# A gated attention and quantised FFN block on one core: the hidden activations of the down product are transposed by DMA instead of by TensorE, with the order of TensorE's work rewritten around it

## The reference

```
x = x + tanh(g_xattn) * xattn(layernorm(x), ctx, ctx)
x = x + tanh(g_ffn)   * ffn(layernorm(x))

xattn: 8 heads of 64. Gates ig, fg from [q, k, v] @ kernel + bias; 
       log_D = cumsum(log_sigmoid(fg)) differences + ig, causal;
       D = exp(log_D - rowmax);  C = (q @ k.T / 8) * D
       h = C / (max(|sum C|, exp(-rowmax)) + eps) @ v;  h = h * rsqrt(mean(h^2) + 1e-6)

ffn:   bitlinear(x, w) = act_quant(x) @ weight_quant(w).T
       act_quant:    per token, round(x * 127 / max|x|) / scale        (whole numbers up to 127)
       weight_quant: round(w / mean|w|) clipped to -1, 0, 1
       g, u = bitlinear(x, w_gate), bitlinear(x, w_up)                  (512 -> 2048)
       h = relu(g)^2 * u
       y = bitlinear(h, w_down)                                        (2048 -> 512)
```

## Time and profile before

| | |
|---|---|
| median of 3 runs | 717.63 us (717.2 to 719.25) |
| the profiled execution | 714.83 us |
| its span | 713.1 us |
| PE busy | 657.5 us, 92% |
| DVE busy | 569.6 us, 80% |
| ACT busy | 424.6 us, 60% |
| POOL busy | 97.9 us, 14% |
| moved by DMA | 63.61 MB, 24.5% of the 16 DMA engines' time on SP's queue |

### The profile page before, as it was taken

One profiled execution on the slowest core, in us unless ns is written; L12 is line 12 of the kernel. 1 busy time (PEld: TensorE's weight loads), 2 busy tenths in 40 slices (PEclk: granted clock), 3 DMA queues, 4 the chain that ended last, 5 costly groups with the idle time before them and its releaser, 6 DMA issues.

```text
span 713.1 us, 13601 instructions
## 1 busy us (share of the span) xinstructions
PE 657.5 (92%) x4245; PEld 436.8 (61%) x4324; DVE 569.6 (80%) x1288; ACT 424.6 (60%) x893; POOL 97.9 (14%) x170
## 2 busy tenths in 40 slices
PE   8895877999999999999999999999999999999797
PEld 5682455575766666574757666665757576666433
DVE  3348756798898979797988979797988889796966
ACT  4254967756656665757566565657575565656542
POOL 1145220110101010101001010101010010101000
PEclk8557767999999999999999999999999999999999
DMA  9904600404113040504031130405040311402000
GB/s 314 382 20 177 206 1 1 163 17 143 37 56 123 15 162 0 177 0 163 15 126 52 49 128 15 162 0 177 0 163 15 117 60 36 143 16 75 2 30 29
DMA packets 45161, 63.61 MB, mean 89 GB/s; under 512 B 1872, under 2 KB 26704, under 8 KB 45136
## 3 DMA queue, kind: packets, MB, share of 16 engines
q1 hardware_dynamic: 43024, 61.19, 24.5%
q10 hardware_dynamic: 2112, 2.11, 0.9%
HBM read 54.77 MB, written 8.52 MB: 89 GB/s over the span
## 4 chain that ended last, share of the span: by engine, by line
PE 46%; DVE 24%; issue 16%; ACT 10%; DMA 2%; POOL 1%; DVEq 1%; SPq 0%; ACTq 0%; POOLq 0%
PE gb L1028 9%; PE ub L1028 8%; PE yb L1051 5%; PE ab L1061 5%; PE tp L1072 3%; PE tp L1074 3%; PE tp L1073 3%; DVE stage L717 3%; DVE dmat L820 2%; DVE ssq L838 2%; PE tp L1097 2%; ACT dmat L524 2%; DMA xs<-in_x 2%; DVE amax L879 2%; PE ab L1039 2%
## 5 line engine op out<-in xcount | busy, mean ns | idle before, releaser
L1028 PE MATMUL gb<-wgT,xqT 128*128 128x512 bf16 x480 | 132.0, 391 | 7.4 <-ACT xqT L505 5.5
L1051 PE MATMUL yb<-wdT,stage 128*128 128x512 bf16 x483 | 134.1, 380 | 2.8 <-ACT stage L498 2.1
L1028 PE MATMUL ub<-wuT,xqT 128*128 128x512 bf16 x497 | 134.2, 388 | 1.8 <-DVE stage L717 0.9
L484 ACT ACTIVATE relu<-gb 128x512 f32<-128x512 f32 x128 | 75.6, 591 | 32.7 <-PE gb L1028 31.7
L717 DVE TENSOR_TENSOR stage<-relu,ub 128x512 f32<-128x512 f32 x128 | 86.1, 682 | 5.3 <-ACT relu L486 5.3
L420 POOL TENSOR_SCALAR_AFFINE_SELECT dmat<-dmat 128x256 f32<-128x256 f32 x128 | 50.0, 415 | 285.1 <-ACT dmat L524 285.1
L1028 PEld LDWEIGHTS ub<-wuT,xqT 128*128 128x128 bf16 x512 | 50.2, 100 | 61.4 <-issue 6.2
L1051 PEld LDWEIGHTS yb<-wdT,stage 128*128 128x128 bf16 x512 | 59.5, 119 | 43.0 <-ACT stage L498 2.0
L532 ACT ACTIVATE ysb<-tp 128x260 f32<-128x260 f32 x64 | 24.8, 387 | 98.0 <-PE tp L1074 98.0
L486 ACT ACTIVATE relu<-relu 128x512 f32<-128x512 f32 x128 | 80.7, 630 | 4.1
L1028 PEld LDWEIGHTS gb<-wgT,xqT 128*128 128x128 bf16 x512 | 48.3, 103 | 54.2 <-issue 8.4
(11 more groups left out here) (114 smaller groups left out, 1090.8 us busy)
## 6 DMA issues: line engine op xcount, KB each, us to landing
dmat<-max_rows SPq DMA_DIRECT2D x14, 1024.0 KB, 5.0
values<-in_ctx_v SPq DMA_DIRECT2D x16, 520.0 KB, 7.5
xs<-in_x SPq DMA_DIRECT2D x16, 512.0 KB, 5.7
cT<-in_ctx_t SPq DMA_DIRECT2D x16, 512.0 KB, 6.7
out<-stage SPq DMA_DIRECT2D x32, 256.0 KB, 2.1
stage<-in_w_gate SPq DMA_DIRECT2D x4, 1024.0 KB, 12.8
stage<-in_w_up SPq DMA_DIRECT2D x4, 1024.0 KB, 17.8
stage<-in_w_down SPq DMA_DIRECT2D x4, 1024.0 KB, 5.2
```

The lines of the kernel that those rows point to most:

```text
L484: nc.scalar.activation(relu[:, c % 2, :], gb[c % 2][:, :], ACT.Relu).then_inc(g_free, 1)
L1028: last = nc.tensor.matmul(bank[c % 2][:, :], xqT[par][:, t, d, :], w[:, d, c * CH:(c + 1) * CH], start=(d == 0), stop=(d == KD - 1))
L1051: done = nc.tensor.matmul(yb[:, :], hqT[:, c, :], wdT[:, c, :], start=(c == 0), stop=(c == KF - 1))
```

## The change

`hq` of a token half is transposed by one DMA that SP issues (`turn_hidden`), [128, 2048] f16 into `hqT[t]`, [128, 16, 128] f16; there are now two tiles `hqT`, one for each half. TensorE's `hidden_transposes` and both `hidden_cols` go. The offset of 1536 stays in `hqT`, and so each `down` begins with one more product, of a tile `offset` (its first row is -1536, the rest 0) with `wsum`, the sums of the columns of `wdT`. `wsum` is made once in step 0, by 16 products with a tile of ones and a copy by ACT (`weight_sums`). DVE's `quantise_hidden` now also waits until the transfer of the half before has read `hq`, and SP's transfer waits for the second of the two quantising instructions and for the `down` that last read its `hqT[t]`.

The order is rewritten with it: TensorE issues all four chunks of a half before it goes on to the products of `down`; for the first half the transposes of q come between chunks (1, 2) and (1, 3), and the 16 gate products stand together between the two halves of `down` instead of one by one among its products. DVE's `output(b, 0)` and the last chunk's multiplication change places with neighbours. In SP's program each transfer stands ahead of the store of the same half.

The diff:

```diff
--- before
+++ after
@@ -134,7 +134,10 @@
         ot = [stage[1][:, FF * 2 + 2 * CH + D * t:FF * 2 + 2 * CH + D * (t + 1)] for t in range(T)]
-        hqT = stage[1][:, FF * 3:FF * 3 + FF // 2].bitcast(BF16).rearrange("p (k s) -> p k s", s=P)
+        hqT = [stage[1][:, FF * 3:FF * 3 + FF // 2].bitcast(F16).rearrange("p (k s) -> p k s", s=P),
+               sb("hqT1", [P, KF, P], F16)]
+        wsum = sb("wsum", [P, D], F16)
+        offset = sb("offset", [P, P], F16)
         hmaxes = sb("hmaxes", [P, T, 2], F32)
...
@@ -357,6 +356,15 @@
+            def turn_hidden(b, t):
+
+                sp.wait_ge(quant_step, QUANT_K * (2 * b + t) + QUANT_K - 1)
+                if not at(b, 0):
+                    alone(sp, sp_passed)
+                    sp.wait_ge(y_full, 2 * b + t - 1)
+                alone(sp, sp_passed)
+                sp.dma_start_transpose(hqT[t][:, :, :], hq[:, :]).then_inc(hq_turned[t], 16)
+
@@ -372,7 +380,9 @@
                 if not at(b, 0):
+                    turn_hidden(b - 1, 1)
                     store(b - 1, 1)
+                turn_hidden(b, 0)
                 store(b, 0)
@@ -380,6 +390,7 @@
             schedule(sp, step)
+            turn_hidden(LAST, 1)
             store(LAST, 1)
...
@@ -490,13 +504,10 @@
-            def hidden_cols(b, t):
-
-                act.wait_ge(a_full[0], hidden_use(b, t) + 1)
-                if not (at(b, 0) and t == 0):
-                    act.wait_ge(y_full, 2 * b + t)
-                nc.scalar.activation(hqT[:, 0:KF // 2, :], abh[0].rearrange("p (k s) -> p k s", s=P), ACT.Copy,
-                                     bias=-MAGIC16).then_inc(a_free[0], 1)
+            def weight_sums():
+
+                act.wait_ge(wsum_full, 1)
+                nc.scalar.activation(wsum[:, :], yb[:, :], ACT.Copy).then_inc(wsum_ready, 1)
@@ -626,8 +637,6 @@
                     magnitudes(2, 0, 4)
-                if prev:
-                    hidden_cols(b - 1, 1)
                 relu_square(b, 0, 2)
@@ -660,10 +669,10 @@
                 relu_square(b, 1, 1)
-                hidden_cols(b, 0)
                 if third:
...
                     sign_weight(2, 3, 4)
+                    weight_sums()
                 if n is not None:
@@ -672,14 +681,13 @@
                     quantise_second(n)
+                relu_square(b, 1, 3)
                 if m is not None:
                     forget_gate(m)
-                relu_square(b, 1, 3)
                 if n is not None:
...
             schedule(act, step)
-            hidden_cols(LAST, 1)
@@ -741,18 +749,14 @@
                     dve.wait_ge(winv_step, WINV[2] + 1)
+                elif t == 0:
+                    dve.wait_ge(hq_turned[1], 16 * b)
+                else:
+                    dve.wait_ge(hq_turned[0], 16 * b + 16)
                 for e in range(2):
...
-
-            def hidden_cols(b, t):
-
-                dve.wait_ge(a_full[1], hidden_use(b, t) + 1)
-                if not (at(b, 0) and t == 0):
-                    dve.wait_ge(y_full, 2 * b + t)
-                nc.vector.tensor_scalar(hqT[:, KF // 2:KF, :], abh[1].rearrange("p (k s) -> p k s", s=P), MAGIC16, None,
-                                        ALU.subtract).then_inc(a_free[1], 1)
@@ -985,22 +986,20 @@
                     quantise_tokens(n, npar)
+                hidden(b, 1, 3)
                 if m is not None:
                     gates_in(m)
+                hidden_max(b, 1, 0)
+                if m is not None:
+                    log_forget(m)
                     output(b, 0, par)
-                    log_forget(m)
-                hidden_max(b, 1, 0)
-                if m is not None:
                     cumulative(m, par)
-                hidden(b, 1, 3)
-                if m is not None:
                     running_max(m, par)
...
             schedule(dve, step)
-            hidden_cols(LAST, 1)
             output(LAST, 1, LAST % 2)
@@ -1029,30 +1028,28 @@
-            def hidden_transposes(b, t):
-                use = hidden_use(b, t)
-                for e in range(2):
-                    pe.wait_ge(quant_step, QUANT_K * (2 * b + t) + QUANT_K - 2 + e)
-                    pe.wait_ge(a_free[e], use)
-                    for s in range(KF // 2):
-                        piece = e * KF // 2 + s
-                        last = nc.tensor.transpose(abh[e][:, s * P:(s + 1) * P], hq[:, piece * P:(piece + 1) * P], identh[:, :])
-                    last.then_inc(a_full[e], 1)
-
-            def down(b, t, first, last, between=None):
+            def weight_sums():
+
+                pe.wait_ge(winv_step, WSUM[2])
+                for c in range(KF):
+                    if c % KD == 0:
+                        pe.wait_ge(w_ready[2], c // KD + 1)
+                    last = nc.tensor.matmul(yb[:, :], warm[:, 0:P], wdT[:, c, :], start=(c == 0), stop=(c == KF - 1))
+                last.then_inc(wsum_full, 1)
+
+            def down(b, t, first, last):
                 for c in range(first, last):
-                    if c == 0 and not (at(b, 0) and t == 0):
-                        pe.wait_ge(o_ready, 2 * b + t)
-                    if c % (KF // 2) == 0:
-                        pe.wait_ge(a_free[c // (KF // 2)], hidden_use(b, t) + 1)
-                    if at(b, 0) and t == 0 and c % KD == 0:
-                        pe.wait_ge(w_ready[2], c // KD + 1)
-                    done = nc.tensor.matmul(yb[:, :], hqT[:, c, :], wdT[:, c, :], start=(c == 0), stop=(c == KF - 1))
+                    if c == 0:
+                        if at(b, 0) and t == 0:
+                            pe.wait_ge(wsum_ready, 2)
+                        else:
+                            pe.wait_ge(o_ready, 2 * b + t)
+                        nc.tensor.matmul(yb[:, :], offset[:, :], wsum[:, :], start=True, stop=False)
+                        pe.wait_ge(hq_turned[t], 16 * b + 16)
+                    done = nc.tensor.matmul(yb[:, :], hqT[t][:, c, :], wdT[:, c, :], start=False, stop=(c == KF - 1))
                     if c == KF - 1:
                         done.then_inc(y_full, 1)
-                    if between is not None:
-                        between(c - first)
@@ -1180,21 +1177,19 @@
                     max_columns(n)
-                chunk(b, 0, 2, par, 0, 1)
-                if prev:
-                    hidden_transposes(b - 1, 1)
-                chunk(b, 0, 2, par, 1, 2)
+                chunk(b, 0, 2, par)
                 chunk(b, 0, 3, par)
-                if prev:
-                    down(b - 1, 1, 0, KF // 2)
                 if n is not None:
...
                 if prev:
-                    down(b - 1, 1, KF // 2, KF)
+                    down(b - 1, 1, 0, KF // 2)
                 if n is not None:
...
                     scores(n, 3, npar)
+                if prev:
+                    down(b - 1, 1, KF // 2, KF)
+                if n is not None:
                     heads_out(n, 0, npar)
@@ -1208,20 +1203,17 @@
                 chunk(b, 1, 1, par)
-                hidden_transposes(b, 0)
                 chunk(b, 1, 2, par)
-                if m is None:
-                    chunk(b, 1, 3, par)
-
-                down(b, 0, 0, KF // 4)
-                if m is None:
-                    down(b, 0, KF // 4, KF)
-                else:
-                    down(b, 0, KF // 4, KF // 2, lambda i: gate_products(m, par, i, i + 1))
+                if m is not None:
                     q_columns(m, par)
-                    down(b, 0, KF // 2, KF // 2 + 1)
-                    down(b, 0, KF // 2 + 1, KF, lambda i: gate_products(m, par, KD + 2 * i, KD + 2 * i + 2))
-                    chunk(b, 1, 3, par)
+                chunk(b, 1, 3, par)
+                if not prev:
+                    weight_sums()
+                down(b, 0, 0, KF // 2)
+                if m is not None:
+                    gate_products(m, par, 0, 2 * T * KD)
+                down(b, 0, KF // 2, KF)
+                if m is not None:
                     cumulative_sum(m)
@@ -1229,7 +1221,6 @@
             schedule(pe, step)
-            hidden_transposes(LAST, 1)
             down(LAST, 1, 0, KF)
```

More of the change, by code:

```diff
@@ L197, in gated_block @@
         quant_step = sem("quant_step")
+        hq_turned = [sem(f"hq_turned{t}") for t in range(T)]
+        wsum_full = sem("wsum_full")
+        wsum_ready = sem("wsum_ready")
         y_full = sem("y_full")
@@ L203, in at @@
             return isinstance(n, int) and n in batches
-        ITER = 8
+        ITER = 6
         STEPS = [(b, b + 1 if b < LAST else None, b + 2 if b + 1 < LAST else None) for b in range(B)]
@@ L216, in bank_order @@
             for b, n, m in STEPS:
-                if b > 0:
-                    uses.append(("hidden", b - 1, 1))
                 if n is not None:
                     uses += [("score", n, kd) for kd in range(KD)]
-                uses.append(("hidden", b, 0))
                 if m is not None:
@@ L225, in bank_order @@
                     uses.append(("token", n, 0))
```

(6 more changed lines are left out.)

2 lines of the change are left out of this document (1 added, 1 removed).

## The result

The changed kernel takes 864.44 us (median of 4 runs, 858.41 to 868.95), the one before beside it 717.41 us (4 runs, 715.05 to 719.25). The ratio is 1.2046, with a 95% interval of 1.1963 to 1.2129: 147 us slower. The profiled execution took 858.41 us, its span is 856.7 us, 143.6 more than before.

A forecast was written before the change was run, and what follows sets the result against it. TensorE was taken to set the pace, DVE close behind. Steps 1 to 13 at 7.3 us each (95), plus 1.0, 3.3 and 2.0, gave 101: span 814, execution 816, median 819 us; range 730 to 890.

The forecast's parts named there:

- The queue: Second half's transfer queues behind SP's loads, landing 13.6 us after the step's start (T0); TensorE resumes at 13.7.
- the rival of a slow transfer: Both transfers run near their piecewise bound, 8.3 us queued and 10.4 alone: 964 us; chance 0.16 with all from 890 up.
- S: Time the second half's transfer adds behind the loads in SP's queue: taken as 1.8 us, high end 8.3.
- A lone transfer: First half's transfer, alone in the queue: hidden at 4.5 us, costing time from 7.0 us on.
- X: Time a transfer alone in the queue should take: 4.5 us, with 3.3 and 10.4 as ends.
- T0 to DVE's output: Step's start to DVE's output of the half before: 18.5 us instead of 12.9, plus 1.6 for the clock.
- DVE's chain behind the output: The 8 us after DVE's output of the half before, where DVE leads: the chain starts only then.
- The clock: After TensorE idles 5.4 us for the second half's transfer, 3.2 us at half clock: 1.6 us lost a step.
- The last stretch of the step: TensorE in the stretch after DVE's output: saves 0.89 us, pays 0.22 + 0.75, so 0.1 us worse.
- The work saved: TensorE's work per step: 1.78 - 0.43 - 0.75 = 0.6 us saved if everything else stays covered.
- The ends: Outside steps 1 to 13: step 0 plus 2.0 us, step 14 1.0, step 15 about 0, last half plus 3.3.
- The sum: Whole run: 13 x 7.3 = 95 us, with 1.0 + 3.3 + 2.0 it is 101; span from 713.1 to 814 us.

The follow-up runs named there:

- gates_mixed: Changed kernel with the first half's `down`, gate products, chunk (1, 3) and DVE's and ACT's moved pieces back in their old order, both transfers still DMA: 831.16 us, ratio 1.1596.

## Why the prediction was right, and where it was short

The forecast was 819 us, the result 864.44. The direction, the place and the mechanism of the wait were right; the clock was mis-sized, and three smaller terms with it. That 864 still lies below the upper end of 890 is in part luck: that end was put there for a transfer slower than 1.8 us, and it was the clock that used the room.

**The queue (right).** Forecast: the second half's transfer lands at T0 + 13.6, 1.8 us behind the loads, and TensorE resumes at 13.7. Measured: 1.8 us behind the loads, and TensorE resumes at 14.02 on average over steps 1 to 13. The wait was forecast at 5.4 us (8.3 to 13.7) and is 4.8 on average. Step 14 waits 0.38 where 0.6 was forecast. Moving the loads showed that it is the queue: 8.9 us to landing became 5.1, again 1.8 us behind what stood ahead. That takes away the rival of a slow transfer: S is the forecast 1.8, far from 8.3, although the transfer does move in small pieces. Before, 1872 packets of the run were under 512 bytes, after it 68,432: 66,560 more for 32 transfers, 2080 each. A piece does not cost here what a packet did in the earlier trace rows.

**A lone transfer (right, a little fast).** X was taken at 4.5 us, with 3.3 and 10.4 as ends; it is 3.7, and hidden in every step but the last, where TensorE waits 0.14 us. The quickest load of as many bytes took 3.3. The rule of the Trainium skill, Advanced Engine Details and Errata, X-Bar Transpose (TRN2), that transposing DMAs on trn2 are as fast as regular ones, agrees with that within 0.4 us. The other figure of the Trainium skill, from DMA: Bandwidth & Descriptors, the table of cycle counts for earlier generations, by which I had estimated 3 us and more of issuing for one transfer, doesn't: SP is in a lone transposing issue for 1.6 us, where a load takes 0.4.

**T0 to DVE's output (right in size).** Forecast 12.9 + 5.6 + 1.6 = 20.1 us, measured 20.87; 7.2 us more a step against 7.9. From the first product to the output it is 6.85, where 4.8 + 1.6 = 6.4 was forecast. What is left of a fall at the start of the step costs nothing by itself, since TensorE waits for the transfer afterwards anyway.

**DVE's chain behind the output (right).** The forecast left it at what it was. Measured from the output to chunk (1, 0): 7.73 us before and 7.74 after.

**The clock (the term that was mis-sized).** The prediction counted one fall behind the wait, 1.6 us a step, 21 us in all. The size of a fall was right, 1.7, and so was its place. But it counted nothing for other falls, and one comes behind the gate products in every step and one behind scores and `heads_out` in 4 of 13. Together they take 5.7 us a step of TensorE's busy time, 75 us in steps 1 to 13, for the 21 forecast; not all of it lengthens the step, since the part before the wait is waited out there. I looked only for what idle time does to the clock. The runs show that it also falls with none: in the kernel before with its gate products put together, with no new wait, it falls right behind them in 11 of 13 steps.

**The last stretch of the step (mis-sized).** Forecast +0.1 us, from 0.89 less, 0.22 more and 0.75 more; measured 18.64 to 20.70, +2.06. The pace of the gate products was right: 32 passes in 3.49 us are 0.109 each, where 0.11 was forecast. What was missing is the fall of 1.7 us behind them. Alone in the kernel before, the regrouping costs 1.3 us a step and 14 us in all. Undone in the kernel after, it gives back 1.4 us a step in this stretch, 18 us. That the whole run won 33 us, close to 13 x (0.75 + 1.7) = 32, is a coincidence: the start and the end gave 8, and the medians lie 6 us further apart than the profiled executions. The changed neighbours on DVE and ACT were undone in the same run, so their share is not separated.

**The work saved (right in sign).** Forecast 0.6 us a step, measured 0.2 by the table above; it counts all busy time at 1.2 GHz as half lost, so it is good to some tenths only. With the gates mixed again and the loads moved up it is 1.0. In the version with the first half alone, 0.89 - 0.22 = 0.67 was to be had, and 0.62 came.

**The ends (too small).** Start: T0 of step 1 moved from 129.16 to 133.28, +4.1 where 2.0 was forecast. ACT's copy to `wsum` waits 1.52 us for the 16 products, and all that DVE does next is 2.1 us later: its x at 120.75 instead of 118.66. That is the forecast part. The rest comes from DVE's new order: its last multiplication of the half, which waits 0.94 us for ACT, and a maximum of 1.21 us now stand ahead of `logf`, which starts at 130.40 instead of 126.34, and for which TensorE waits:

```profile
130.62 0.60 PE L1103 MATMUL tp<-logf,upper 128*128 128x8 f32 x2 [4.44 <-DVE logf L798]
```

Step 14: +1.9 for 1.0. Last half: +3.3 was forecast; from the start of the last quantising to the end of the span it is 856.7 - 840.30 = 16.4 us instead of 713.1 - 703.54 = 9.6, +6.8. The rows of the end:

```profile
842.52 0.34 SPq L370 DMA_DIRECT2D out<-stage  x1
843.04 1.60 SPq L366 DMA_TRANSPOSE hqT<-hq  x1
```

```profile
842.55 0.61 PE L1048 MATMUL yb<-wsum,offset 128*128 128x512 f16 x1 [2.61 <-DVE stage L767]
846.85 6.48 PE L1050 MATMUL yb<-wdT,hqT 128*128 128x512 bf16 x16 [3.69 <-DMA hqT<-hq]
```

`hq` is ready at 840.30 + 1.42 = 841.72, but the transfer stands on SP behind the store of the first half, which waits for DVE's output; that is 1.3 us. The 16 products then run at half clock, 6.48 us instead of the 3.61 of the earlier trace rows.

**The sum.** By the profiled executions: 13 x 10.0 = 130 for 95; 4.1 for 2.0; 1.9 for 1.0; and 7.7 for the rest of the end, for 3.3. That is 143.7 for 101, and the span is 856.7 for 814. The median lies 6.0 above the profiled execution, where I had put 2.8.

**Open.** In the version with loads moved up and gates mixed, falls remain in 11 of 13 steps, all of them behind scores and `heads_out` with a wait of 0.6 us for `dmat`. No run separates whether this wait, the short wait for the transfer or the new order of scores and products brings them. The 3.1 us of idle time a step of that version are 0.9 for `logf`, 0.8 for `dmat`, 0.7 for the transfer and smaller ones; what they would be with the new order and no transfer to wait for wasn't tried.

## What to carry to other kernels

Before a product's operand is moved from an engine to a DMA, look at what stands in the same queue when the operand becomes ready: here the same 512 KB transfer was free where the queue was empty (0.62 us a step gained) and cost some 5 us of waiting behind 2.6 MB of loads. When small products are taken out from between large ones, count their pace, and also look at the granted clock behind them; here a fall cost 1.7 us and the pace 0.75. Where a change has two halves that meet different neighbours, try each alone: one half of this one was the fastest kernel, 707.44 us.

## What the runs showed that I had not expected

- TensorE's clock fell from 2.4 to 1.2 GHz behind a stretch in which the engine was busy all the time, 3.5 us of f32 products with 16 columns, with no idle time ahead of it. The same 16 products spread among products of 512 columns brought no fall.
- It also fell behind scores and `heads_out` with a single wait of 0.6 us among them, in 13 of 13 steps of `gates_mixed`. A new order of small products is to be checked for this too.
- SP stays longer in a transposing issue the more is in the queue: 7.01 us in one instruction behind 2.6 MB, 2.96 behind 1 MB, 1.6 with an empty queue, against 0.4 for a load. Everything that SP has to do after it waits for it.
- Behind other transfers the same 512 KB land 1.8 us after the last of them, whether 1 or 2.6 MB stand ahead.
- A transfer of 128 x 2048 f16 is 2080 packets, all under 512 bytes, and still lands in 3.7 us.
- 20 needless products in a wait did not make the kernel slower but, by the medians, 12.8 us faster (2 and 4 runs, 845.58 to 857.67 against 858.41 to 868.95), since the clock stayed up behind them.
